# Memory attention and a routed feed-forward on eight cores: gram and scores in one product, q turned after its projection, the factor chain moved, VectorE evicting one gathered bank, four norms of the second half made ahead

## The chip, the cores and the metric

One Trainium2 chip, the program on all 8 cores, each core with its own two of the 16 sequences (4096 tokens of 1024 values) and all weights; no core talks to another. The metric is device microseconds of the slowest core. An engine names its queue here: PE is TensorE, PEld its weight load, DVE VectorE, ACT ScalarE, POOL GpSimd, SP SyncE.

## What is computed

```
x = x + attn(layernorm(x)) ; x = x + ffn(layernorm(x))

attn: q, k, v = x Wq', x Wk', x Wv' in 16 heads of 64; k normalised per head
  for each chunk of 64 tokens, with a memory M (64x64) per head:
    scores = q k' / 8, causal mask, softmax;  attn_out = softmax v
    chunk_out = attn_out + 0.1 * q M
    then for each token of the chunk: M = M - alpha (M k) k' + beta v k'
  out = concat(chunk_out) Wo'

ffn: tokens in groups of 16; for each of 64 experts the token of the group
     with the highest logit is chosen (0/1 matrix perm)
  sel = perm' x ; inner = relu(sel f1 + bias) ; inter = inner f2 ; out = perm inter
```

## The kernel before

**Attention (phase_a).** A step handles 128 rows: 64 tokens of each of the core's two sequences. The token recurrence of M is solved by chunk: gram (`gram`, -alpha k k') is masked by POOL into A[0] and B[0], nilpotent matrices whose powers PE makes by squaring (`power_a`, `power_b`, five and four products of 32 small 64x64 matmuls, all into PSUM psX, each copied out by ACT). DVE adds the identity (`plus_eye`, AI[k]) and PE multiplies them into W (`factor` 0 to 5, into psW, each copied out by DVE as W or, the last, Wf). `k_by_h`, `state_h` and `state_m` use and update the state H and M in psY. `scores`, exp, mask, `row_sums` and `values` are the softmax attention, also through psY, and `queries` adds q M. The projections of k, v and q and the output projection (`wo_part`) share the banks psD0 and psD1, as do the transposes of x and k (`x_turn`, `k_turn`, through psT, which is psD0).

The loop has 35 steps, i = -1 to 34, software-pipelined: in step i the projections belong to tile i, `gram` to tile i-1, powers, factors, scores and queries to u = i-2, and state and output projection to e = i-3. All engines are programmed by hand with semaphores; each executes its own list in order, so a wait holds all that is behind it. A projection half is 8 matmuls of 512 columns, except q, which was made with the weight as stationary operand: 64 matmuls of 128 columns, so that q comes out feature-major (q_fm) and needs no transpose. A weight load goes with each matmul ("pair" below).

PE's list of a full step before, in order: k half 0; power_a 1; factor 5 (e); k half 1; power_b 1; factor 0; state_h; v half 0; power_a 2; factor 1; state_m; half of v half 1; x_turn; power_b 2; k_by_h; rest of v half 1; power_a 3; factor 2; scores; q half 0; power_b 3; q half 1; factor 3; row_sums; gram; wo half 0; power_a 4; half of wo half 1; k_turn; power_b 4; queries; rest of wo half 1; power_a 5; factor 4; values. That is 834 pairs: 112 of projections, 16 of transposes, 2 of row sums and 22 groups of 32 small ones. POOL squares k, scales it, masks gram and scores, makes Pn and ka, and in between issues eight DMAs a step that cast the feed-forward weights f1, f2 to bf16 in DRAM.

**Feed-forward (phase_b).** Two halves of 16 tiles. A gather stage makes, for each tile, the layer norm (`choice_stats` and `choice_norm` on DVE, `choice_ln` on ACT), the transposed tile (`y_turn`, yf), logits, the choice matrix (perm, psel) and four gathers of 1024 columns into P0 and P1 in turn, which ACT alone evicts into R (L1070); gather q waits until copy q-2 is done. An expert stage runs 32 pairs of experts (`layer1`, relu, `layer2`; DVE and ACT evict a half each). A rows stage transposes R back, scatters, adds x1 and stores. Before, the norm of tile 16 and the statistics of tile 17 were made in the rows stage of the first half, and tiles 0 and 1 likewise at the end of attention.

## Time and profile before

| | us |
|---|---|
| median of 3 runs | 1457.8 (1455.39 to 1459.32) |
| profiled execution, time | 1463.14 |
| its span (slowest core, core 0) | 1460.0 |
| PE busy | 1176.9 (81%) |
| DVE busy | 959.4 (66%) |
| ACT busy | 814.2 (56%) |
| POOL busy | 686.8 (47%) |
| attention | 0 to about 1067 |
| gather, experts, rows of the first half | 1067 to 1150, to 1210, to 1265 |
| the same of the second half | 1265 to 1345, to 1402, to 1460 |

The page gives one execution, on its slowest core. Busy shares are averages over stages with different limits, so each stage is read for itself: which wait ends last there. An idle time put down to "issue" is one in which the engine waited for nothing that the profile shows. The first and last steps of attention stand apart from the full ones: the first wait for weights, the last have no projections.

### The profile page before, as it was taken

To read this page: it belongs to the slowest core of one execution; us is meant where nothing else is said; L and a number is where in the kernel's file an instruction comes from. 1 tells how busy PE (TensorE), PEld (TensorE's weight loads), DVE (VectorE), ACT (ScalarE), POOL (GpSimd) and SP (SyncE) were. 2 spreads that over 40 slices of the span, in tenths; PEclk is the share of its full clock that TensorE was granted. 3 is DMA by queue.
4 is the path that set the end of the run, shared out by engine and by line. 5 is a ranking of instruction groups with operands and counts; after the bars stand their busy time and mean duration, and the time that the engine had idled before them with its cause. 6 is when DMAs were issued, how large, how long until landed. Compare 5 with 4: busy or idle time off the path is not lost. (4 is left out here: it accounts for less than half of the span.)

```text
span 1460.0 us, 72310 instructions; the slowest of 8 cores (1445.7 to 1460.0 us)
## 1 busy us (share of the span) xinstructions
PE 1176.9 (81%) x31168; PEld 768.4 (53%) x31168; DVE 959.4 (66%) x1325; ACT 814.2 (56%) x1187; POOL 686.8 (47%) x566
## 2 busy tenths in 40 slices
PE   1578888888888988888888888885577879777788
PEld 0355565555555555555555555553444466543665
DVE  2266776676767777667765666765667467873776
ACT  0155555555555555555555555563339866489775
POOL 3176666766667666676666766676201000011000
PEclk9789999999999999999999999996558789888999
DMA  9812222222222222222222222113124285741958
GB/s 155 145 39 43 45 46 53 47 43 45 46 53 47 45 47 46 52 46 49 45 45 45 50 43 42 27 30 74 30 73 152 77 273 157 235 153 42 279 144 241
DMA packets 75173, 122.35 MB, mean 84 GB/s; under 512 B 13408, under 2 KB 38000, under 8 KB 74864
## 3 DMA queue, kind: packets, MB, share of 16 engines
q1 hardware_dynamic: 48128, 92.30, 21.1%
q0 software_dynamic: 26736, 25.44, 13.2%
q8 instruction: 254, 4.16, 1.2%
q14 instruction: 55, 0.45, 0.1%
HBM read 117.93 MB, written 41.94 MB: 110 GB/s over the span
## 5 line engine op out<-in xcount | busy, mean ns | idle before, releaser
L807 DVE CAST W<-psW 128x1024 bf16<-128x1024 f32 x160 | 195.1, 1219 | 100.5 <-PE psW L602 98.5
L403 ACT CAST B<-psX 128x1024 bf16<-128x1024 f32 x128 | 129.8, 1014 | 87.4 <-PE psX L570 87.4
L803 DVE TENSOR_TENSOR AI<-A,eye 128x1024 bf16<-128x1024 bf16 x160 | 118.5, 757 | 44.2 <-ACT A L399 43.1
L1058 POOL TENSOR_TENSOR psel<-permT_sb,gmask_sb 128x256 bf16<-128x256 bf16 x32 | 19.8, 620 | 269.3 <-DVE permT_sb L1287 244.1
L519 PE MATMUL psD<-xnf,wq_sb 128*128 128x128 bf16 x2048 | 132.7, 224 | 14.3 <-DMA wq_sb<-wqT 7.9
L486 PE MATMUL psD<-wk_sb,xnf 128*128 128x512 bf16 x512 | 128.8, 397 | 18.3 <-DMA wk_sb<-wkT 13.1
L399 ACT CAST A<-psX 128x1024 bf16<-128x1024 f32 x128 | 130.2, 1017 | 19.0 <-PE psX L570 18.8
L495 PE MATMUL psD<-wv_sb,xnf 128*128 128x512 bf16 x512 | 128.8, 385 | 13.0 <-DMA wv_sb<-wvT 11.7
L545 PE MATMUL psD<-wo_sb,o_fm 128*128 128x512 bf16 x512 | 131.9, 393 | 1.3 <-issue 1.0
L519 PEld LDWEIGHTS psD<-xnf,wq_sb 128*128 128x128 bf16 x2048 | 120.5, 100 | 19.0 <-issue 16.2
L358 POOL TENSOR_TENSOR Ms_sb<-M_sb,b 128x1024 bf16<-128x1024 bf16 x31 | 68.7, 2215 | 128.8 <-DVE M_sb L851 128.8
L1070 ACT CAST R<-P 128x1024 bf16<-128x1024 f32 x128 | 120.6, 1022 | 5.9 <-PE P L1148 5.5
L1297 DVE CAST R<-P 128x512 bf16<-128x512 f32 x128 | 81.6, 687 | 44.6 <-PE P L1175 44.4
L570 PEld LDWEIGHTS psX<-A,B 64*64 64x64 bf16 x5120 | 59.1, 111 | 96.2 <-issue 95.4
L602 PE MATMUL psW<-W,AI 64*64 64x64 bf16 x5120 | 80.1, 199 | 29.0 <-issue 21.3
L365 POOL TENSOR_TENSOR PT<-PT,mj 128x1024 bf16<-128x1024 bf16 x32 | 68.1, 2129 | 73.7 <-ACT PT L441 73.7
L570 PE MATMUL psX<-A,B 64*64 64x64 bf16 (+1 forms) x5120 | 77.8, 196 | 26.2 <-issue 11.9
L354 POOL TENSOR_TENSOR sq_sb<-kraw 128x1024 f32<-128x1024 f32 x32 | 60.7, 1896 | 76.4 <-ACT kraw L407 58.3
L411 ACT CAST vt<-psD 128x512 bf16<-128x512 f32 x64 | 37.5, 586 | 100.8 <-PE psD L495 100.8
L374 POOL TENSOR_TENSOR A<-g_sb,mlo 128x1024 bf16<-128x1024 bf16 x32 | 68.0, 2125 | 52.7 <-ACT g_sb L462 52.7
L807 DVE CAST Wf<-psW 128x1024 bf16<-128x1024 f32 x32 | 39.2, 1225 | 77.3 <-PE psW L602 77.3
L486 PEld LDWEIGHTS psD<-wk_sb,xnf 128*128 128x128 bf16 x512 | 46.8, 100 | 74.5 <-issue 29.2
(136 smaller groups left out, 2594.5 us busy)
## 6 DMA issues: line engine op xcount, KB each, us to landing
ring<-f1d SPq DMA_DIRECT2D x64, 256.0 KB, 4.0
ring<-f2d SPq DMA_DIRECT2D x64, 256.0 KB, 5.5
out<-ring SPq DMA_DIRECT2D x64, 256.0 KB, 4.0
xy<-x SPq DMA_DIRECT2D x68, 128.0 KB, 2.4
f1d<-f1w POOLq DMA_DIRECT2D x128, 64.0 KB, 2.5
f2d<-f2w POOLq DMA_DIRECT2D x128, 64.0 KB, 2.7
x1d<-x1b SPq DMA_DIRECT2D x64, 128.0 KB, 1.8
xy<-x1d SPq DMA_DIRECT2D x32, 256.0 KB, 3.1
```

The lines of the kernel that those rows point to most:

```text
L399: s.copy(A[k][:], psX[:, 0:1024]).then_inc(s_a, 1)
L403: s.copy(B[k][:], psX[:, 0:1024]).then_inc(s_b, 1)
L486: ins = t.matmul((psD0, psD1)[hf][:, :], xn_fm[i % 2][:, kc * 128:(kc + 1) * 128], wk_sb[:, kc * 1024 + hf * 512:kc * 1024 + hf * 512 + 51 ...
L495: ins = t.matmul((psD0, psD1)[hf][:, :], xn_fm[i % 2][:, kc * 128:(kc + 1) * 128], wv_sb[:, kc * 1024 + hf * 512:kc * 1024 + hf * 512 + 51 ...
L519: ins = t.matmul((psD0, psD1)[hf][:, (oc % 4) * 128:(oc % 4) * 128 + 128], wq_sb[:, kc * 1024 + oc * 128:kc * 1024 + oc * 128 + 128], xn_f ...
L545: ins = t.matmul((psD0, psD1)[hf][:, :], o_fm[:, oc * 128:(oc + 1) * 128], wo_sb[:, oc * 1024 + hf * 512:oc * 1024 + hf * 512 + 512], star ...
L570: ins = t.matmul(psX[c:c + 64, hr * 64:hr * 64 + width], left[k][r:r + 64, hr * 64:hr * 64 + 64], right[k][r:r + 64, hr * 64:hr * 64 + width],
L602: ins = t.matmul(psW[c:c + 64, hr * 64:hr * 64 + 64], AI[k][r:r + 64, hr * 64:hr * 64 + 64], w_old, start=True, stop=True, tile_position=( ...
L803: v.tensor_tensor(heads(AI[k][:, :]), heads(A[k][:, :]), by_mask(eye2), ALU.add).then_inc(s_ai, 1)
L807: v.tensor_copy((Wf if k == 5 else W[k % 2])[:], psW[:, 0:1024]).then_inc(s_w, 1)
L1070: s.copy(gather_place(n, q), P[q % 2][:, 0:1024].rearrange("p (h cb r) -> p h cb r", h=2, cb=4)).then_inc(s_ga, 1)
L1297: v.tensor_copy(place(2 * p)[:, 4 * hf:4 * hf + 4, :, :], half_tiles(P[u % 3][:, 0:512])).then_inc(s_iv, 1)
```

## The change

- **Gram and scores** become one group, `gram_and_scores(j)`, with j = i-1: k is the stationary operand and the moving one is 128 columns wide, 64 of -alpha k and 64 of q, from a joint buffer kaq. The result fills psX and psY together (psXY). ACT copies the even slots to g_sb and takes exp of the odd ones into PT, now two buffers, a step earlier than before. The group also waits for the turned q and for the logarithm of the row sums (s_lden), and power_a 4 and queries wait for the exp.
- **q** is projected as k and v are (16 matmuls of 512 columns), copied token-major to q_tm by ACT, transposed in `q_turn` (8 matmuls, through psD1) and copied to q_fm by DVE, which `wo_part` of half 1 and the next step's k half 1 wait for.
- **The factor chain** starts later: factors 0 to 3 run in step u+2, factors 4 and 5 in the next. PE's list of a full step after: k half 0; power_a 1; factor 4 (e); k half 1; power_b 1; factor 5 (e); v half 0; power_a 2; state_h; half of v half 1; power_b 2; state_m; rest of v half 1; x_turn; power_a 3; k_by_h; q half 0; power_b 3; factor 0; row_sums; half of q half 1; k_turn; gram_and_scores; factor 1; rest of q half 1; half of wo half 0; power_a 4; factor 2; q_turn; rest of wo half 0; power_b 4; queries; wo half 1; power_a 5; factor 3; values.
- **DVE's list** of a full step after: AI5 (e); evict factors 3 and 4; plus_eye 0; evict factor 5; plus_eye 1; H; the sum of squares kss (before, it stood behind factor 2, much later) and its maximum; M; xnf; plus_eye 2; RHS; stats of x; evict factor 0; k_fm; plus_eye 3; evict factor 1; normal (xn_tm); evict factor 2; q_fm; x1 half 0; plus_eye 4; x1 half 1.
- **At the end of attention** statistics and norms of tiles 0 to 3 are made (before: norm of 0, statistics of 0 and 1).
- **Gather**: ACT evicts gathers 0 to 2 whole and half of gather 3; DVE evicts the other bank of gather 3, at the end of its iteration, and PE waits for it before the next tile's gather 1.
- **Norms ahead**: in the first half's expert stage, between pairs 16 and 28, DVE and ACT make statistics and norms of tiles 16 to 19 (NPRE = 4), with their loads on SP among the weights; what stood in the rows stage is gone.

The diff, cut to its core (the lists of PE and DVE stand above in words; `o_copy` is the old copy of o_fm, now at the head of the next step):

```diff
-        q_fm = [sb(pa, f"qf{b}", [128, 1024]) for b in range(3)]
+        q_tm = sb(pa, "q_tm", [128, 1024])
+        kaq_fm = [sb(pa, f"kaq{b}", [128, 2048]) for b in range(3)]
-        ka_fm = [sb(pa, f"ka{b}", [128, 1024]) for b in range(3)]
-        PT = sb(pa, "PT", [128, 1024])
+        PT = [sb(pa, f"PT{b}", [128, 1024]) for b in range(2)]
-        psX = ps(pa, "psX", [128, 1024])
+        psXY = ps(pa, "psXY", [128, 2048])
-        psY = ps(pa, "psY", [128, 1024])
+        psX, psY = psXY[:, 0:1024], psXY[:, 1024:2048]
+        psT1 = psD1[:, :].bitcast(BF16)
+        gram_scores = psXY[:, :].rearrange("p (h b c) -> p h b c", b=2, c=64)
+        ka_fm = [kaq[:, 0:1024] for kaq in kaq_fm]
+        q_fm = [kaq[:, 1024:2048] for kaq in kaq_fm]
...
-                if 0 <= u < NT:
-                    g.wait_ge(s_exp, u + 1)
-                    g.tensor_tensor(heads(PT[:, :]), heads(PT[:, :]), by_mask(mj), ALU.mult).then_inc(s_ptm, 1)
...
+                    if u > 0:
+                        g.wait_ge(s_po, u)
+                    g.tensor_tensor(Pn[:], PT[u % 2][:], rden[:], ALU.mult).then_inc(s_pn, 1)
...
+                    cast(u, 6)
+                    g.wait_ge(s_exp, i)
+                    g.tensor_tensor(heads(PT[(i - 1) % 2][:, :]), heads(PT[(i - 1) % 2][:, :]), by_mask(mj),
+                                    ALU.mult).then_inc(s_ptm, 1)
...
-                if proj:
-                    v_half(i, 1)
-                if solve:
-                    power_a(u, 3)
-                    s.wait_ge(s_psc, u + 1)
-                    s.activation(PT[:], psY[:, 0:1024], AF.Exp, scale=0.125).then_inc(s_exp, 1)
                 if proj:
                     s.wait_ge(s_kmax, i + 1)
                     s.activation(rk[:], kss[:], AF.Ln).then_inc(s_rk, 1)
                     s.wait_ge(s_rk, 2 * i + 1)
                     s.activation(rk[:], rk[:], AF.Exp, scale=-0.5).then_inc(s_rk, 1)
+                    v_half(i, 1)
+                if solve:
+                    power_a(u, 3)
+                if proj:
                     q_half(i, 0)
                 if solve:
                     power_b(u, 3)
-                if i + 2 < NT:
-                    ln_steps(i + 2)
+                    s.wait_ge(s_pden, u + 1)
+                    if u > 0:
+                        s.wait_ge(s_pn, u)
+                    s.activation(rden[:], psY, AF.Ln).then_inc(s_lden, 1)
                 if i == -1:
                     s.wait_ge(s_const, NCONST)
                     s.activation(ab_sb[:, :], ab_sb[:, :], AF.Exp, scale=-1.0).then_inc(s_esig, 1)
+                if 0 <= j < NT:
+                    s.wait_ge(s_pg, j + 1)
+                    s.copy(heads(g_sb[:, :]), gram_scores[:, :, 0, :]).then_inc(s_g, 1)
+                    s.activation(heads(PT[j % 2][:, :]), gram_scores[:, :, 1, :], AF.Exp, scale=0.125).then_inc(s_exp, 1)
-                if solve:
-                    s.wait_ge(s_pden, u + 1)
-                    s.activation(rden[:], psY[:, 0:1024], AF.Ln).then_inc(s_lden, 1)
-                if 0 <= i - 1 < NT:
-                    s.wait_ge(s_pg, i)
-                    s.copy(g_sb[:], psX[:, 0:1024]).then_inc(s_g, 1)
                 if solve:
                     s.wait_ge(s_lden, u + 1)
                     s.activation(rden[:], rden[:], AF.Exp, scale=-1.0).then_inc(s_rec, 1)
+                if i + 2 < NT:
+                    ln_steps(i + 2)
+                if solve:
                     power_a(u, 4)
                     power_b(u, 4)
-                    s.wait_ge(s_po, u + 1)
-                    s.copy(o_fm[:, :].rearrange("p (a s c) -> p s a c", a=8, s=2),
-                           psY[:, 0:1024].rearrange("p (s a c) -> p s a c", s=2, a=8)).then_inc(s_o, 1)
                 if i >= NT + 1:
-                    choice_ln(s, env, i - NT - 1)
+                    choice_ln(s, env, 2 * (i - NT - 1))
+                    choice_ln(s, env, 2 * (i - NT - 1) + 1)
...
+                    if i > 3:
+                        t.wait_ge(s_x1, 2 * (i - 3) - 1)
                 else:
                     if i > 0:
-                        t.wait_ge(s_q, 2 * i)
+                        t.wait_ge(s_qfm, i)
...
-            def q_half(i, hf):
...
-                for oc in range(4 * hf, 4 * hf + 4):
-                    for kc in range(8):
-                        ins = t.matmul((psD0, psD1)[hf][:, (oc % 4) * 128:(oc % 4) * 128 + 128],
-                                       wq_sb[:, kc * 1024 + oc * 128:kc * 1024 + oc * 128 + 128],
-                                       xn_fm[i % 2][:, kc * 128:(kc + 1) * 128],
-                                       start=(kc == 0), stop=(kc == 7))
-                ins.then_inc(s_pq, 1)
+                for kc in range(lo, hi):
+                    ins = t.matmul((psD0, psD1)[hf][:, :], xn_fm[i % 2][:, kc * 128:(kc + 1) * 128],
+                                   wq_sb[:, kc * 1024 + hf * 512:kc * 1024 + hf * 512 + 512],
+                                   start=(kc == 0), stop=(kc == 7))
+                if hi == 8:
+                    ins.then_inc(s_pq, 1)
...
-                if i > 2:
-                    t.wait_ge(s_x1, 2 * (i - 3) + 1)
...
+            def q_turn(i):
+
+                t.wait_ge(s_q, 2 * i + 2)
+                for oc in range(8):
+                    ins = t.transpose(psT1[:, oc * 128:(oc + 1) * 128], q_tm[:, oc * 128:(oc + 1) * 128], ident_bf[:])
+                ins.then_inc(s_tq, 1)
...
                     t.wait_ge(s_o, e + 1)
-                    if e + 3 < NT:
-                        t.wait_ge(s_q, 2 * (e + 3) + hf + 1)
-                    else:
-                        t.wait_ge(s_kfm, NT)
+                    t.wait_ge((s_kfm, s_qfm)[hf], min(e + 4, NT))
+                    if e + 3 >= NT:
                         t.wait_ge(s_x1, 2 * e)
...
-            def gram(j):
+            def gram_and_scores(j):
+
                 t.wait_ge(s_ka, j + 1)
+                t.wait_ge(s_qfm, j + 1)
                 if j > 0:
                     t.wait_ge(s_b, 4 * (j - 1) + 3)
+                    t.wait_ge(s_lden, j)
                 for h in range(NH):
                     r, hr = (h % 2) * 64, hrow(h)
                     for s in range(2):
                         c = (h // 2) * 128 + s * 64
-                        ins = t.matmul(psX[s * 64:s * 64 + 64, hr * 64:hr * 64 + 64],
-                                       ka_fm[j % 3][r:r + 64, c:c + 64], k_fm[j % 3][r:r + 64, c:c + 64],
+                        ins = t.matmul(psXY[s * 64:s * 64 + 64, hr * 128:hr * 128 + 128], k_fm[j % 3][r:r + 64, c:c + 64],
+                                       kaq_fm[j % 3][:, :].rearrange("p (b x) -> p b x", b=2)[r:r + 64, :, c:c + 64],
                                        start=True, stop=True, tile_position=(r, s * 64))
...
                     t.wait_ge(s_g, u + 2)
+                    t.wait_ge(s_exp, u + 2)
...
-            def scores(u):
-                t.wait_ge(s_rhs, u + 1)
-                t.wait_ge(s_q, 2 * u + 2)
...
-                ins.then_inc(s_psc, 1)
-
             def row_sums(u):
                 t.wait_ge(s_ptm, u + 1)
+                t.wait_ge(s_rhs, u + 1)
...
                     load_pair(32 * half + p)
+                    if half == 0 and 16 <= p < 16 + NPRE:
+                        load_y(p)
...
-                    if half == 0 and 2 <= tl < 2 + NY:
-                        load_y(16 + tl - 2)
+                    if half == 0 and 2 <= tl < 2 + NY - NPRE:
+                        load_y(16 + NPRE + tl - 2)
...
-                s.copy(gather_place(n, q),
-                       P[q % 2][:, 0:1024].rearrange("p (h cb r) -> p h cb r", h=2, cb=4)).then_inc(s_ga, 1)
+                h = 1 if q == 3 else 2
+                s.copy(gather_place(n, q)[:, 0:h, :, :], gathered_ps(q)[:, 0:h, :, :]).then_inc(s_ga, 1)
...
+                    if half == 0 and 17 <= p < 17 + 3 * NPRE and p % 3 == 2:
+                        choice_ln(s, env, 16 + (p - 17) // 3)
...
+                if n > 0 and q == 1:
+                    t.wait_ge(s_gv, n)
...
+                t.wait_ge(s_gv, 16 * (half + 1))
...
-                    if j + 3 < 16:
+                    if NPRE <= j + 3 < 16:
                         choice_norm(v, env, n + 3)
...
+                    if 0 <= j - 2:
+                        v.wait_ge(s_pg, 4 * (n - 2) + 4)
+                        v.tensor_copy(gather_place(n - 2, 3)[:, 1, :, :], gathered_ps(3)[:, 1, :, :]).then_inc(s_gv, 1)
...
+                    if half == 0 and 16 <= p < 16 + 3 * NPRE and p % 3 == 1:
+                        choice_stats(v, env, 16 + (p - 16) // 3)
+                    if half == 0 and 18 <= p < 18 + 3 * NPRE and p % 3 == 0:
+                        choice_norm(v, env, 16 + (p - 18) // 3)
...
-                    if half == 0 and tl in (8, 10):
-
-                        choice_stats(v, env, 16 + (tl - 8) // 2)
-                    if half == 0 and tl == 13:
-                        choice_norm(v, env, 16)
```

## Rows read from the trace of the kernel before

**Rows 1.** Busy time by stretch: us, PE, PEld, DVE, ACT, POOL (instructions), PEclk, DMA, GB/s.
```profile
232.00:901.00 669.00, 577.37 (x18347) 376.57 (x18346) 463.26 (x550) 363.23 (x506) 451.20 (x352) 0.99 0.24 47
```

**Rows 2.** What PE waited for, 232 to 901 us: total us, times, longest.
```profile
PE psW L602 <- issue: 16.1, 22, 1.3
PE psX L570 <- issue: 15.7, 20, 1.5
...
PE psY L640 <- DVE M_sb L851: 6.5, 12, 0.6
PE psX L570 <- ACT g_sb L462: 6.1, 14, 0.5
...
PE psD L507 <- issue: 0.3, 1, 0.3
```

**Rows 3.** DMA queues, 232 to 901 us.
```profile
q8 instruction: 148, 2.42, 1.5%
```

**Rows 4.** Timeline of PE in one step: start, us, line, tiles, count, idle before.
```profile
511.73 0.26 PE L625 MATMUL psY<-Wf,RHS 64*64 64x64 bf16 x8 [0.95 <-issue]
...
515.85 0.43 PE L602 MATMUL psW<-W,AI 64*64 64x64 bf16 x29 [0.20 <-issue]
516.18 0.45 PE L652 MATMUL psY<-qf,kf 64*64 64x64 bf16 x32
516.56 1.96 PE L519 MATMUL psD<-xnf,wq_sb 128*128 128x128 bf16 x32
518.45 0.45 PE L570 MATMUL psX<-B,A 64*64 64x64 bf16 x32
520.76 1.95 PE L519 MATMUL psD<-xnf,wq_sb 128*128 128x128 bf16 x32 [1.86 <-issue]
...
527.20 0.61 PE L532 MATMUL psD<-ident_bf,kt 128*128 128x128 bf16 x8
527.74 0.45 PE L570 MATMUL psX<-B,A 64*64 64x64 bf16 x32
```

**Rows 5.** Timeline of ACT and DVE in the same step.
```profile
518.27 1.21 DVE L868 TENSOR_REDUCE kss<-sq_sb 128x16 f32<-128x1024 f32 x1
...
522.36 0.20 ACT L395 ACTIVATE rstd<-rstd 128x1 f32<-128x1 f32 x1
...
524.36 0.80 DVE L795 TENSOR_SCALAR xn_tm<-xy,mv,rstd 128x1024 bf16<-128x1024 f32 x1
524.64 1.01 ACT L462 CAST g_sb<-psX 128x1024 bf16<-128x1024 f32 x1
525.53 1.07 ACT L465 ACTIVATE rden<-rden 128x1024 f32<-128x1024 f32 x1
...
528.39 0.68 DVE L894 COPY kf<-psD 128x1024 bf16<-128x1024 bf16 x1
```

**Rows 6.** Timeline of attention's last step.
```profile
1054.43 1.23 DVE L807 CAST Wf<-psW 128x1024 bf16<-128x1024 f32 x1 [1.07 <-PE psW L602]
```

**Rows 7.** Costliest groups of the page: an eviction of one bank.
```profile
L1297 DVE CAST R<-P 128x512 bf16<-128x512 f32 x128 | 81.6, 687 | 44.6 <-PE P L1175 44.4
```

**Rows 8.** What PE waited for in the gather stage of the first half, 1085 to 1150 us.
```profile
PE P L1148 <- ACT R L1070: 12.1, 29, 0.7
```

**Rows 9.** Timeline of the first tiles of the first gather stage.
```profile
1074.11 0.68 DVE L117 BATCH_NORM_STATS2 bst_y<-xy 128x6 f32<-128x512 bf16 x1
...
1074.48 1.03 PE L1115 MATMUL P<-ident_bf,xy 128*128 128x128 bf16 x8 [2.67 <-DVE yf L1271]
```

**Rows 10.** Timeline late in the second gather stage's fill: an iteration of DVE.
```profile
1283.37 0.63 DVE L136 TENSOR_SCALAR xy<-xy,mv_y,rstd_y 128x1024 bf16<-128x1024 bf16 x1 [0.33 <-ACT rstd_y L130]
...
1287.50 0.56 DVE L136 TENSOR_SCALAR xy<-xy,mv_y,rstd_y 128x1024 bf16<-128x1024 bf16 x1 [0.40 <-ACT rstd_y L130]
```

**Rows 11.** Busy time of the first half's expert stage, columns as in rows 1.
```profile
1150.00:1210.00 60.00, 48.17 (x1032) 37.89 (x1032) 39.77 (x63) 44.61 (x98) 0.00 (x0) 0.84 0.70 213
```

**Rows 12.** Timeline of PE in the first half's rows stage.
```profile
1242.45 0.62 PE L1202 MATMUL P<-ring,pselT_sb 128*64 128x512 bf16 x4 [0.83 <-DVE ring L1303]
```

196 lines of the change are left out of this document (108 added, 88 removed).

## Prediction

> **What bounds the kernel now.** I read the page's slices first (attention is 1067 of 1460 us, PE eight or nine tenths busy), then the busy time of the 22 full steps between 232 and 901 us, then who PE waited for in them, the DMA queues of the same stretch, one step instruction by instruction, and last the stages of the feed-forward. A full step takes 669/22 = 30.4 us, and PE is busy for 577.4/22 = 26.2 of them; DVE is busy for 21.1, POOL for 20.5, ACT for 16.5 [rows 1]. So PE is the bound, but 4.2 us a step are idle. The table of waits says why: 13 of its rows, of which the two largest and the smallest stand, are "issue", together 67.1 us or 3.05 a step; all waits for other engines make about 20 us, 0.9 a step, the largest M_sb (6.5) and g_sb (6.1) [rows 2].
>
> What "issue" is comes out of two more views. The instruction queue moved 148 packets, 2.42 MB, so about 16 KB each, one every 669/148 = 4.5 us, and 18,347 pairs / 148 = 124 pairs of weight load and matmul go with each [rows 1, 3]. In the timeline the gaps stand at just that distance: from the end of the gap at 515.85 to the next come 29+32+32+32 = 125 pairs, in 4.9 us, and 4.1 us passed since the gap before [rows 4]. After slow pairs (projections of 512 columns) there is no gap, after quick ones there is. I read this as PE running out of instructions: a packet takes some 4.2 us (estimated from the two distances, 4.1 and 4.9, the lower weighing more because waits of other kinds lengthen some), and where 124 pairs take less work than that, PE waits.
> The Trainium skill, page "Runtime: NRT & Kernel Launch", section "Instruction fetch mechanics", says that engines are refilled in 16 KiB blocks of 256 instructions, and there the trace agrees (148 packets of 16 KB); it also says that this fetch is hidden because instructions issue slower than blocks arrive. The gaps of up to 2.4 us every 124 pairs speak against that, and by the page they would have another cause and stay; that is the last rival.
>
> **The change, attention.** *Work of PE in a full step.* q: 64 matmuls in two halves of 1.89 us become 16 of 512 columns; k's and v's halves take about 1.84, so -0.1. q_turn adds 8 transposes, 0.54 from the start of k_turn to what follows [rows 4]. Scores and gram, each 32 small matmuls in 0.38 us (516.18 to 516.56 [rows 4]), become 32 of 128 columns: not below one group (0.38), not much above two (0.76, the same columns), as far as the trace has a like; I take 0.6, nearer to the upper end because the columns are twice as many, so -0.16. Sum +0.3 (0.0 to +0.45): 26.5 us.
> *Instructions.* 48 pairs of q and 32 of scores go, 8 come: 834 becomes 762, or 6.73 packets a step 6.15. This is the gain. Before, work and outside waits per packet were (26.2+0.9)/6.73 = 4.0 us; after, (26.5+2.4)/6.15 = 4.7, 0.65 more. If each gap shrinks by 0.65, of the 87 gaps that I listed in the stretch (65.9 us in all, from 0.2 to 2.4) those beyond keep 21 us together, 0.95 a step instead of 3.05.
> *New waits.* From the end of gram_and_scores (call it 0) ACT copies g (1.0), takes exp (1.0), copies q half 1 (0.6), takes exp of rden (1.07), does ln (two short ones, 0.6 with their hand-over), then A4 (1.0) [rows 5]. With 0.2 us of hand-over A4 is done at 5.6, and behind it on PE stand power_b 4, queries and wo half 1. PE's own work up to there (factor 1, half of q, half of wo, power_a 4, factor 2, q_turn, half of wo) is 4.6. So 1.0 us is lost. Then DVE: normal can start only after ln (4.6), 0.8; eviction of factor 2, 1.2; q_fm, 0.7: wo half 1 gets its bank at 7.3 to 7.4, where PE is ready at 6.6. Another 0.75. In the first part of the step kss (1.2 and about 0.6 for the maximum) now stands ahead of M on DVE: k_by_h, and the q projection behind it through xnf, wait for M until about 12.4 of the step where PE arrives at about 11.2; about 1.3 with xnf. In all 3.1 us if PE is never held by anything else; before, such waits were halved by the fetch gaps that fell ahead of them, so I take 2.4 (0.9, as before, to 3.1). The other moves cost nothing: DVE has 21.1+0.7 of 30 us, hidden by PE's work; POOL's kt, Pn, B0 and the mask are ready by the walk at least 2 us early; ACT's work is the same. SP's loads of x wait for q copies that come about as before, three tiles ahead.
> *Sum.* 26.5+2.4+0.95 = 29.8, with joints 29.7, against 30.4: -0.7 us, times 30 full steps = **-21 us**. Ends: waits of 0.9 give 28.4, -2.0 a step, -60; all 3.1 give 30.4, nothing.
>
> *End of attention.* The last step now begins with the eviction of factor 3 and has factor 4 before factor 5: one more product of 0.9 and one more eviction of 1.2 in a chain in which DVE and PE wait for one another [rows 6]; +2. The exp of scores leaves the last solving step's chain, -1. Two more norms and two more statistics on DVE lie beside wo's products and the last store, +0.5. Together **+1.5** (-1 to +4).
>
> **The change, feed-forward.** *Fill of the gather stages.* With four norms ready, y_turn of tile 2 doesn't wait 2.67 us behind norm and statistics of DVE (two of 0.68 and an aggregate before each copy of yf) [rows 9]; with a little for tile 3, -4 in the first half, and -2.5 in the second, where one norm was ready already.
> *Evictions.* PE waited 12.1 us in 65 for ACT's copies [rows 8]. Only the waits behind gather 3 go, where ACT now needs 0.6 for 1.0; gather 0 waits for gather 2's whole copy as before. -0.25 for some 12 tiles a half at PE's low clock. But DVE gets 0.69 for its bank [rows 7]: its iteration of 4.1 us in the fast part, with some 0.4 idle [rows 10], becomes 4.4, and DVE takes ACT's place as the bound there: +0.3 for some 6 tiles of the second half. Last tiles of each half, without statistics, gain 0.4 four times. Together -5 (-12 to +3).
> *Expert stage.* Four statistics of 1.6 us and four norms of 0.55, 8.7 us of DVE work, fall into 12 of 32 pairs, some 22 us. DVE is busy 39.8 of 60 [rows 11], evenly 15 in those 22, so there is room for 7; but the evictions come in strict turn and the layer 2 buffers let DVE lag by one pair only. Ends 1.5 and 8.7; I take +4. SP's four loads among the weights hide, since the ring is ten pairs deep.
> *Rows stage.* The statistics held PE by 0.83 us, twice, of which one stands [rows 12]: **-1.7**.
> Sum of the feed-forward: -4-2.5-5+4-1.7 = **-9** (-18 to +3).
>
> **Total.** -21+1.5-9 = -28.5 us. Against the profiled execution's own 1463.1 (3.1 outside its span) that is 1434.6; this execution lies 5.3 above the median of 1457.8, so for the median I say **1429 us**.
>
> **Rivals.**
> *Full relief.* The waits in the step stay at 0.9, because the remaining gaps and other work cover ACT's chain: 28.4 a step, -60 +1.5 -9, about 1390 us. For it: before, g and M cost 0.3 each where their walk says 0.5 to 0.6. Against: two chains of 0.75 to 1.0 with no slack stand close together.
> *The chain takes it all.* Waits of 3.1 and gaps of 0.95: 30.4 a step, only the rest remains: about 1451.
> *Slower, by DVE's list.* kss stands ahead of M and waits for POOL's squares; M holds k_by_h, xnf and through it all of q. It decides from the point at which POOL's square ends later than H, about 2 us of slack by my walk; then each us of POOL's lateness is one of PE's, and normal's wait for ln does the same later in the step. With 1.5 us more, 31.2 a step: +24+1.5-7 = 1476. POOL's 20.5 us of 30.4 speak against it.
> *Slower, the gaps aren't the fetch.* Then they stay at 3.05: with 26.5 and 1.8 of waits 31.3 a step, +27+1.5-7, about 1479. The even distance of 124 pairs speaks against it. This is what the Trainium skill's rule on instruction fetch comes to here.
>
> **How the numbers follow.** Forecast 0.48 (its own range 1414 to 1445), full relief 0.22, the chain takes it all 0.13, slower by DVE 0.10, gaps not the fetch 0.07. The range of 1387 to 1456 holds the first three with their spreads and leaves out the slower two and a little below. A measurement of this kernel can tell about 0.3% from no change. Faster by more: 0.48+0.22 and two thirds of the third, 0.78; slower 0.16; within 0.3% the rest, 0.06.
>
> **What would show it.** Right: full steps of 29.7 us; the instruction queue at about 135 packets for 22 steps; "issue" near 1 us a step; on PE new waits for ACT's A4 before power_b 4 and for DVE's q_fm before wo; gram_and_scores in 0.5 to 0.7 us; fewer waits for R's copies in the gather; DVE without idle time in the middle of the first expert stage. Wrong: "issue" still 3 us a step; waits for M_sb over 1 us a step; a group of 128 columns of 0.85 us or more; a gather stage that is longer because PE waits for DVE's bank.

## The result: 54 us slower, all of it in attention

| | before | after |
|---|---|---|
| median of the runs, us | 1456.6 | 1510.9 |
| range of the runs, us | 1452.8 to 1459.3 | 1508.0 to 1512.5 |
| profiled execution, own time / span, us | 1463.1 / 1460.0 | 1511.1 / 1509.5 |
| last half of x1 starts (end of attention), us | 1064.7 | 1130.9 |
| from there to the end, us | 395.3 | 378.6 |
| one full step of attention, us | 30.5 | 33.1 |

The ratio is 1.037 (95% interval 1.0348 to 1.0392). All times and ratios here and below are of the fast runs: some executions of any kernel run some per cent longer, with a lower granted clock on the cores of one die, and are left out. A step is here the mean distance between two starts of GpSimd's first mask, `A<-g_sb,mlo`, between 230 and 930 us; all steps below are measured so. Attention grew by 66 us, where the forecast took 19.5 off it, and the feed-forward shrank by 17, where the forecast took 9. Most of what follows is about the 66.

Page of the kernel after, the costliest groups (busy us, mean ns of one, idle before):

```profile
L824 DVE TENSOR_TENSOR AI<-A,eye 128x1024 bf16<-128x1024 bf16 x160 | 271.0, 1694 | 1.3 <-ACT A L410 1.3
...
L568 PE MATMUL psD<-wo_sb,o_fm 128*128 128x512 bf16 x512 | 139.4, 410 | 50.6 <-DVE kaq L917 50.6
```

The same instruction, plus_eye, is line 803 of the kernel before, where its row in the groups reads:

```profile
L803 DVE TENSOR_TENSOR AI<-A,eye 128x1024 bf16<-128x1024 bf16 x160 | 118.5, 757 | 44.2 <-ACT A L399 43.1 <-POOL A L374 1.0
```

The shape, the count and the operands are the same, yet one takes 1694 ns instead of 757. No part of the change touches it except its place.

Busy time of the kernel after in the stretch of [rows 1], with the same columns; what PE waited for in it, as in [rows 2]; and the instruction queue, as in [rows 3]:

```profile
232.00:901.00 669.00, 550.16 (x15387) 310.51 (x15385) 557.69 (x524) 338.57 (x468) 408.70 (x324) 0.95 0.22 43
```

```profile
PE psD L568 <- DVE kaq L917: 37.4, 20, 2.1
PE psXY L596 <- DVE AI L857: 26.9, 20, 1.9
PE psW L629 <- DVE W L828: 16.0, 21, 0.8
PE psXY L596 <- ACT A L410: 7.4, 16, 0.6
PE psXY L667 <- DVE M_sb L879: 5.8, 15, 0.7
PE psW L629 <- issue: 4.6, 9, 1.0
PE psXY L596 <- issue: 4.0, 8, 1.0
```

```profile
q8 instruction: 125, 2.05, 1.3%
```

Per step (22.0 of them before, 20.2 after, from 762 pairs a step):

| us a step | before | forecast | after |
|---|---|---|---|
| PE busy | 26.2 | 26.5 | 27.2 |
| issue | 3.05 | 0.95 | 0.68 |
| waits for other engines | 0.9 | 2.4 | 4.9 |

So the relief came: issue rows sum to 13.7 us in place of 67.1. That they are even smaller than forecast isn't a gain by itself, since a wait for an engine hides an instruction packet that arrives in it. What ate the relief is the third line of the table, and of its 98.5 us in the stretch 80.3 are three waits for VectorE: for q's turned copy (37.4), for the fifth AI (26.9), for an eviction of psW (16.0).

Where VectorE's time went is seen in one step. Timeline of VectorE, GpSimd and TensorE after the copy of A4 (start us, duration us, engine and line, out<-in, idle before):

```profile
500.43 2.14 POOL L383 TENSOR_TENSOR Pn<-PT,rden 128x1024 bf16<-128x1024 bf16 x1 [0.28 <-ACT rden L483]
...
500.88 2.23 DVE L816 TENSOR_SCALAR xn_tm<-x,mv,rstd 128x1024 bf16<-128x1024 f32 x1 [2.04 <-ACT rstd L406]
...
503.03 1.21 DVE L828 CAST W<-psW 128x1024 bf16<-128x1024 f32 x1
503.23 2.13 POOL L386 TENSOR_TENSOR B<-g_sb,mup 128x1024 bf16<-128x1024 bf16 x1
504.17 0.68 DVE L917 COPY kaq<-psD 128x1024 bf16<-128x1024 bf16 x1
504.76 0.67 DVE L835 TENSOR_TENSOR x1b<-xy,psD 128x512 bf16<-128x512 f32 x1
504.99 3.31 PE L568 MATMUL psD<-wo_sb,o_fm 128*128 128x512 bf16 x8 [1.60 <-DVE kaq L917]
505.29 0.55 POOL L354 DMA_DIRECT2D f2d<-f2w  x1
505.36 5.03 DVE L824 TENSOR_TENSOR AI<-A,eye 128x1024 bf16<-128x1024 bf16 x1
...
505.85 2.13 POOL L389 TENSOR_TENSOR PT<-PT,mj 128x1024 bf16<-128x1024 bf16 x1
507.93 1.89 POOL L395 TENSOR_TENSOR kaq<-kf,nega 128x1024 bf16<-128x1024 bf16 x1
...
510.31 0.67 DVE L835 TENSOR_TENSOR x1b<-xy,psD 128x512 bf16<-128x512 f32 x1
```

Normal takes 2.23 us where [rows 5] has 0.80, and ends 0.54 after GpSimd's Pn. plus_eye 4 takes 5.03 where 0.68 is usual, and ends 0.57 after GpSimd's last multiply (507.93 + 1.89 = 509.82 to 510.39). The evictions in between, whose input is in PSUM, have their usual 1.21 and 0.68 beside GpSimd's B. Between 232 and 901 us plus_eye takes over 2 us in 20 instances, one in each step, all of 5.02 to 5.04, and it is plus_eye 4 each time. Behind it the second half of x1 and the fifth AI are late, so are product 5 of psX and the eviction of factor 3. In this step PE has waited 1.60 us, and behind the wait its granted clock falls from the 2.4 to about the 1.2 GHz level: the eight products of wo take 3.31 us, for 1.89 of eight like ones at the full level. Busy time of these 3.2 us, columns as before, with 0.55 as the granted clock (it is 1.00 in the 7 us ahead of them):

```profile
505.00:508.20 3.20, 3.20 (x8) 0.94 (x8) 3.20 (x2) 0.00 (x0) 3.19 (x4) 0.55 0.34 67
```

This doesn't follow every wait. The same wait stands in all 20 steps (1.2 to 2.1 us); behind it wo's products take 3.16 to 3.43 us in six of them and 1.89 in fourteen. The clock also falls behind the wait for the fifth AI, in twelve steps. Over the whole stretch it is 0.95, for the 0.99 of [rows 1].

### The profile page after: what moved, and what is told of

It reads as the page before. It is cut to its first block and busy times, and to the rows that moved or that the text cites. A ratio compares the mean times of both kernels' runs of the same rounds, so it can differ in the third digit from the quotient of the medians.

```text
span 1509.5 us, 68111 instructions; the slowest of 8 cores (1491.9 to 1509.5 us)
## 1 busy us (share of the span) xinstructions
PE 1193.4 (79%) x28864; PEld 704.3 (47%) x28864; DVE 1155.3 (77%) x1389; ACT 809.9 (54%) x1187; POOL 677.6 (45%) x566
## 3 DMA queue, kind: packets, MB, share of 16 engines
q1 hardware_dynamic: 48128, 92.30, 19.5%
## 5 line engine op out<-in xcount | busy, mean ns | idle before, releaser
L824 DVE TENSOR_TENSOR AI<-A,eye 128x1024 bf16<-128x1024 bf16 x160 | 271.0, 1694 | 1.3 <-ACT A L410 1.3
L414 ACT CAST B<-psXY 128x1024 bf16<-128x1024 f32 x128 | 129.8, 1014 | 57.5 <-PE psXY L596 57.4
L410 ACT CAST A<-psXY 128x1024 bf16<-128x1024 f32 x128 | 129.3, 1010 | 48.9 <-PE psXY L596 48.7
L539 PE MATMUL psD<-wq_sb,xnf 128*128 128x512 bf16 x512 | 128.7, 385 | 11.7 <-DMA wq_sb<-wqT 6.8
L365 POOL TENSOR_TENSOR kt<-kraw,rk 128x1024 bf16<-128x1024 f32 x32 | 61.2, 1913 | 128.8 <-ACT rk L460 128.8
L1108 ACT CAST R<-P 128x1024 bf16<-128x1024 f32 (+1 forms) x128 | 110.0, 906 | 8.4 <-PE P L1187 6.4
L596 PE MATMUL psXY<-A,B 64*64 64x64 bf16 (+1 forms) x5120 | 74.7, 194 | 50.3 <-DVE AI L857 41.4
L596 PEld LDWEIGHTS psXY<-A,B 64*64 64x64 bf16 x5120 | 57.4, 110 | 111.0 <-issue 107.4
L629 PE MATMUL psW<-W,AI 64*64 64x64 bf16 x5120 | 76.9, 199 | 33.8 <-DVE W L828 29.3
L418 ACT COPY kraw<-psD 128x512 f32<-128x512 f32 x64 | 37.4, 586 | 117.0 <-PE psD L507 117.0
L568 PEld LDWEIGHTS psD<-wo_sb,o_fm 128*128 128x128 bf16 x512 | 49.2, 103 | 107.2 <-issue 68.1
L596 PEld LDWEIGHTS psXY<-B,A 64*64 64x64 bf16 x4096 | 49.0, 114 | 80.7 <-issue 80.5
```

What stands on the lines that cost most here:

```text
L410: s.copy(A[k][:], psX).then_inc(s_a, 1)
L414: s.copy(B[k][:], psX).then_inc(s_b, 1)
L539: ins = t.matmul((psD0, psD1)[hf][:, :], xn_fm[i % 2][:, kc * 128:(kc + 1) * 128], wq_sb[:, kc * 1024 + hf * 512:kc * 1024 + hf * 512 + 51 ...
L568: ins = t.matmul((psD0, psD1)[hf][:, :], o_fm[:, oc * 128:(oc + 1) * 128], wo_sb[:, oc * 1024 + hf * 512:oc * 1024 + hf * 512 + 512], star ...
L596: ins = t.matmul(psX[c:c + 64, hr * 64:hr * 64 + width], left[k][r:r + 64, hr * 64:hr * 64 + 64], right[k][r:r + 64, hr * 64:hr * 64 + width],
L629: ins = t.matmul(psW[c:c + 64, hr * 64:hr * 64 + 64], AI[k][r:r + 64, hr * 64:hr * 64 + 64], w_old, start=True, stop=True, tile_position=( ...
```

## The experiments

Theory (the **meeting**): a VectorE instruction that takes its inputs from SBUF stands still as long as GpSimd works on SBUF, through several of GpSimd's instructions if they follow closely. The change moved normal, plus_eye 4 and GpSimd's mask of PT into one another. Rivals: the new operand waits themselves (**waits**: A4, q's copy, the order of VectorE's list), or the new shapes and tiles. The Trainium skill, page "SBUF — State Buffer", section "Who interferes with whom", has the mechanism as a rule: VectorE and GpSimd share one pair of SBUF ports, taken as an exclusive lock, and an instruction of VectorE with two SBUF inputs contends with a GpSimd one that reads SBUF, as does a copy or tensor_scalar in a two-port mode with GpSimd. Both kinds that stretched here are of its list: plus_eye has two inputs in SBUF (0.68 us alone, 5.03 here), and normal is a tensor_scalar from SBUF to SBUF (0.80 and 2.23). In which mode normal ran, no trace shows.

All rows below named "group" are of the list of costliest groups, the waits are those of PE between 232 and 901 us. e1 to e8 were measured on one chip, e9 and e10 on a second, e11 and e12 on a third; the kernel before, run beside them, took 1457, 1453 and 1457 us. A difference between two chips is therefore given below by the ratios to the kernel before as well. Summary:

| run | edit | us | step us |
|---|---|---|---|
| e1_mask_short | after, mask of PT left out but for one head | 1448.1 | 30.8 |
| e2_eye4_late | after, plus_eye 4 behind x1's second half | 1492.5 | 32.0 |
| e3_norm_early | after, ln and normal earlier | 1484.1 | 33.3 |
| e4_both | e2 and e3 | 1518.4 | 33.1 |
| e7_eye4_next | after, plus_eye 4 one step on | 1454.7 | 30.7 |
| e6_no_meeting | e7 and e3 | 1439.1 | 30.4 |
| e9_pool_waits | e6, GpSimd held back | **1393.9** | 28.9 |
| e12_eye0_too | e9, plus_eye 0 earlier as well | 1405.9 | 29.4 |
| e8_more_pairs | e6, 96 pairs a step more | 1465.1 | 31.1 |
| e5_before_ffn | before, feed-forward part alone | 1451.7 | 30.5 |
| e10_before_meets | before, plus_eye 4 beside GpSimd | 1607.9 | 35.5 |
| e11_before_held | e10, GpSimd held back | 1492.9 | 31.9 |

**e1_mask_short** leaves the causal mask of 15 of 16 heads out (so the scores of these aren't masked):

```diff
-g.tensor_tensor(heads(PT[(i-1)%2]), heads(PT[(i-1)%2]), by_mask(mj), ALU.mult)
+g.tensor_tensor(PT[(i-1)%2][:, 0:64], PT[(i-1)%2][:, 0:64], mj[:, :], ALU.mult)
```

> The changed kernel, but POOL masks only one head of PT (64 of 1024 columns), so the causal mask is left out for the rest; every wait stays. Theory A (VectorE operations that read two SBUF tiles, or one in a fast mode, can't run while POOL reads SBUF): plus_eye 4, 5.0 us in the changed kernel, becomes about 2.9, and a full step gets 1 to 1.8 us shorter, about 1465 us. Theory B (only the new order of waits costs: normal behind ln, q_fm behind normal, M behind kss): nobody waits late for this mask, so plus_eye 4 and the time stay, 1511 us.

1448.1 us, one run, 63 less than the kernel after and 17 less than expected. The group of plus_eye falls to a mean of 964 ns, and plus_eye 4 takes 0.68 us in every step of the stretch, though VectorE's list is untouched; I had expected 2.9. Work was removed, so this only shows that GpSimd's list stretches VectorE; the wait for q's copy stays, since normal still lies beside Pn:

```profile
L824 DVE TENSOR_TENSOR AI<-A,eye 128x1024 bf16<-128x1024 bf16 x160 | 154.3, 964 | 1.3 <-ACT A L410 1.3
```

```profile
PE psD L568 <- DVE kaq L917: 38.8, 21, 2.1
```

**e2_eye4_late**, **e3_norm_early** and **e4_both** move VectorE's instructions within the step:

```diff
 # e2: VectorE                     # e3: VectorE
 x1_half(e, 0)                     k_fm copy
-plus_eye(u, 4)                    +normal(i + 2)
 x1_half(e, 1)                     plus_eye(u, 3); factor(u, 1)
+plus_eye(u, 4)                    -normal(i + 2)
                                   # and on ScalarE ln_steps(i + 2) ahead of g's copy
```

> The changed kernel with plus_eye 4 moved on VectorE behind the second x1 half; nothing left out. Theory A: it meets only the end of POOL's ka, takes about 1.2 us instead of 5.0, while x1's second half waits for PE anyway; AI5 comes 0.7 us earlier a step, about 1490 us. Theory B: no change or slower, 1511 to 1520, since the same work stands in the same list.

> The changed kernel with ln on ACT directly behind rden's logarithm and normal on VectorE directly behind k_fm, ahead of plus_eye 3, so before POOL starts A0; nothing left out. Theory A: normal takes 0.8 instead of 2.24 us, no wait of 2.2 us for ln stands on VectorE, q_fm is there when PE wants it (wait of 1.9 us a step gone), about 1440 us. Theory B: the wait goes too but normal's duration is the same as before the move; 1460 to 1480 us.

> The changed kernel with both moves, plus_eye 4 behind the second x1 half and ln and normal early; nothing left out. Theory A: attention steps near 29.5 us, 1415 to 1430 us in all, below the kernel before. Theory B: no better than the early norm alone.

1492.5, 1484.1 and 1518.4 us. e2 took the time expected, though plus_eye 4 did not: it takes 1.1 to 2.8 us, 2.0 on average, for 1.2. In e3 normal is back at 0.81 us and the wait for q's copy is gone, but the time fell by 27 only, not by 71: plus_eye 4, which now starts 2.6 us earlier behind gram_and_scores, meets three instructions of GpSimd (B, PT, the scaling of k) in place of two and takes 7.5 us in most steps. Its profile (an execution of 1493.8 us) holds a test of its own: the 20 steps in which plus_eye 4 takes 7.3 to 7.6 us last 31.8 to 35.0 us, the eight in which it takes 0.7 to 1.3 last 26.8 to 30.0. And of the eight cores, with the same work each, the one with 12 such meetings between 232 and 901 us has the shortest span (1443.2) and the two with 17 and 18 the longest (1492.3 and 1487.3). Groups of e3, and its largest wait:

```profile
L824 DVE TENSOR_TENSOR AI<-A,eye 128x1024 bf16<-128x1024 bf16 x160 | 304.1, 1901 | 1.3 <-ACT A L410 1.3
```

```profile
PE psXY L596 <- DVE AI L857: 57.6, 18, 4.1
```

e4, expected at 1415 to 1430, was slower than the kernel after: behind x1 plus_eye 4 still meets the mask and the scaling (4.83 us at 528.59), now later in the step. Both misses have one cause: I moved the instruction by its old durations, to where GpSimd had been, and GpSimd's list moved along. No place that I tried inside this tail of GpSimd's multiplies was safe.

**e7_eye4_next** and **e6_no_meeting** put plus_eye 4 into the next step, ahead of the eviction of factor 4 (PE's waits for AI count accordingly, as in all runs below that move it); e6 also has e3's edit.

```diff
-if solve: plus_eye(u, 4)
 # next step
 factor(e, 3)
+plus_eye(e, 4)
 factor(e, 4)
```

> The changed kernel with the move of plus_eye 4 alone, ln and normal where the change has them. Theory A: the waits for AI5 and W go (2 us a step), the wait for q_fm (1.9 us a step) stays, since normal still meets Pn for 2.24 us and waits for ln: 1440 to 1460 us. Theory B: 1500 or more.

> The changed kernel, nothing left out: ln and normal early as in e3, and plus_eye 4 moved into the next step between the evictions of factors 3 and 4, when POOL has done ka and has nothing until the squares of k. Theory A (VectorE's two-input and fast SBUF operations wait while POOL reads SBUF): plus_eye 4 takes 0.7 us in every step, steps are 28 to 29 us as in the steps of e3 in which they don't meet, 1395 to 1420 us in all, below the kernel before. Theory B (VectorE's order and load as such): factor 4 now waits for one more operation of VectorE, no better than e3 at its best, 1450 or more.

1454.7 us (ratio to before 0.9984, 0.9945 to 1.0023) and 1439.1 (0.9852, 0.9816 to 0.9889). One instruction moved gives back the whole loss of the change, 56 of 54 us: in e7 plus_eye 4 takes 0.79 us on average, while the wait for q's copy stays (40.9 us in the stretch). e6 is faster than both kernels, but 19 us above its expectation, and its trace says why: without normal's delay VectorE comes earlier and plus_eye 4 meets GpSimd's tail again, with 2.8 us on average and 3.4 at most. The 16 us between e7 and e6 aren't normal's stretch alone, since e3's edit also takes a wait of about 2 us for ln off VectorE's list; no run parts the two. Waits of e6, largest row, and timeline:

```profile
PE psW L629 <- DVE AI L824: 35.4, 20, 2.6
```

```profile
505.82 2.14 POOL L389 TENSOR_TENSOR PT<-PT,mj 128x1024 bf16<-128x1024 bf16 x1
...
507.39 2.97 DVE L824 TENSOR_TENSOR AI<-A,eye 128x1024 bf16<-128x1024 bf16 x1
...
507.90 1.90 POOL L395 TENSOR_TENSOR kaq<-kf,nega 128x1024 bf16<-128x1024 bf16 x1
```

**e9_pool_waits** leaves VectorE as in e6 and moves GpSimd instead, by one wait:

```diff
 cast(u, 6)
 g.wait_ge(s_exp, i)
+if 0 <= u < NT: g.wait_ge(s_ai, 6 * u + 6)   # plus_eye 4 done
 g.tensor_tensor(heads(PT[...]), ...)          # the mask, then the scaling of k
```

> As e6_no_meeting, and GpSimd holds its mask of PT and the scaling of k back until VectorE's plus_eye 4 is done, so that no GpSimd work lies beside that instruction; the same instructions on every engine, GpSimd has one wait more a step. Theory (a VectorE instruction with inputs in SBUF is stretched by GpSimd work beside it): plus_eye 4 takes 0.68 instead of 2.97 us, the product behind it starts 2.3 us earlier, the clock's dip behind it goes, so 1.3 to 2.5 us less in each of 30 steps than e6's 1439: 1365 to 1410, likeliest 1395. Theory that e6 is already held by something else (the operand waits as such): within 10 us of 1439. If GpSimd's delayed list comes to set the end (scaling of k needed by gram_and_scores, some 16 us later): over 1450.

1393.9 us, ratio 0.959 (0.9549 to 0.963): 45 us below e6 (38 by the ratios, 0.985 to 0.959) and 4.1% below the kernel before, for one added wait. The rival of the operand waits, within 10 us of 1439, is out. This is the cleanest test in the changed kernel: the same instructions on every engine, VectorE's and TensorE's in the same order. Busy time, the largest waits, and plus_eye 4 with GpSimd behind it:

```profile
232.00:901.00 669.00, 600.58 (x17607) 348.59 (x17605) 535.89 (x603) 382.39 (x533) 471.77 (x370) 0.99 0.24 48
```

```profile
PE psXY L669 <- DVE M_sb L882: 13.4, 20, 3.3
PE psXY L654 <- DVE H_sb L872: 11.9, 16, 2.0
PE psW L631 <- DVE W L830: 10.5, 19, 2.4
```

```profile
510.74 0.68 DVE L826 TENSOR_TENSOR AI<-A,eye 128x1024 bf16<-128x1024 bf16 x1
...
511.57 2.12 POOL L391 TENSOR_TENSOR PT<-PT,mj 128x1024 bf16<-128x1024 bf16 x1 [2.10 <-DVE AI L826]
```

With 23.1 steps in the stretch PE works 26.0 us a step, waits 0.9 for instructions and 1.8 for engines. The clock is back at 0.99. Not every meeting is gone: plus_eye 0, 1 and 2 take 1.3 to 1.6 us on average here, for the 0.68 of an undisturbed one.

**e12_eye0_too** tried to free plus_eye 0 as well, which takes 2.02 us at 514.07 in e9 beside the scaling of k.

```diff
 plus_eye(e, 4)
+plus_eye(u, 0)
 factor(e, 4)
-plus_eye(u, 0)
 # GpSimd waits for 6 * u + 7
```

> As e9_pool_waits, and plus_eye 0 (which met the scaling of k there, 2.02 us) stands right behind plus_eye 4, ahead of the eviction of factor 4, in time in which VectorE waited for TensorE (1.51 us); GpSimd waits for both. Theory of the meeting: it takes 0.68, the last eviction and the adding to H come up to 1.3 us earlier, TensorE's waits for H (11.9 us, 16 times in 669 us) and M (13.4, 20) shrink: 0.3 to 1 us a step below e9's 1394, 1362 to 1386. Rival: these waits are set by the chain of products itself, then within 5 us of 1394.

1405.9 us, 12 slower than e9 (8 by the ratios, 0.965 and 0.959, whose intervals overlap), where 8 to 32 less were expected: a miss for both theories as I had put them. The timeline shows the meeting moved, not gone. GpSimd, held for one instruction more, gets to k's scaling and the square later, and in several steps plus_eye 1, which stands ahead of the adding to H, lands beside the square:

```profile
489.09 3.23 DVE L826 TENSOR_TENSOR AI<-A,eye 128x1024 bf16<-128x1024 bf16 x1
...
489.85 1.90 POOL L361 TENSOR_TENSOR sq_sb<-kraw 128x1024 f32<-128x1024 f32 x1
...
492.24 1.21 DVE L873 TENSOR_TENSOR H_sb<-H_sb,psXY 128x1024 bf16<-128x1024 bf16 x1
...
493.59 0.45 PE L654 MATMUL psXY<-Wf,RHS 64*64 64x64 bf16 x32 [1.47 <-DVE H_sb L873]
```

That this makes up the difference isn't shown. Over the run plus_eye takes less than in e9 (a mean of 1068 ns for 1145), and PE's waits for H, M and W in the stretch sum to 37.4 us for 35.8. Why e12 isn't faster stays open.

**e10_before_meets** and **e11_before_held** take the question into the kernel before, with nothing of the change. e10 moves plus_eye 4 behind the fifth AI; e11 is e10 with GpSimd's B and scaling of k held until plus_eye 4 is done.

```diff
 # e10, VectorE                      # e11 adds, GpSimd
-plus_eye(u, 4)   # behind x1 half 0   cast(u, 6)
 AI[5] += eye                        +g.wait_ge(s_ai, 6 * u + 6)
+plus_eye(u, 4)                        B <- g_sb by mup
 factor(u, 4)
```

> The kernel before with one instruction moved: VectorE's plus_eye 4 stands behind the fifth AI (about 502.4 in its trace) where GpSimd's B and ka run (501.3 to 505.3), instead of behind the first half of x1, where GpSimd is idle or issues a DMA. Nothing of the change is in it. Theory: plus_eye 4 takes 2.5 to 3.2 us there, the mean of the AI<-A,eye group rises from 757 ns to 1150 to 1300, and the fourth eviction is 3 to 4 us later, so 1 to 3 us a step: 1490 to 1540. Theory that the stretch comes with something of the change (the shared tile of ka and q, two PT tiles, the order of the other instructions): plus_eye 4 stays at 0.7 us and only the lost head start is paid, 1460 to 1490.

> As e10_before_meets (the kernel before, plus_eye 4 behind the fifth AI), and GpSimd holds B and ka back until plus_eye 4 is done. VectorE's and TensorE's lists are those of e10, so the lost head start of plus_eye 4 is paid in both and only the meeting is gone. Theory of the meeting: plus_eye 4 back at 0.68 us (4.42 in e10), TensorE's wait for it from 5.2 us a step to about 1.5, some 3.7 us a step and 30 steps less than e10's 1608: 1480 to 1510. Theory that the late place of the instruction, not its length, costs e10's 155 us: within 20 us of 1608.

1607.9 us (ratio 1.1053) and 1492.9 (1.0233). Groups and waits of e10, then of e11:

```profile
L803 DVE TENSOR_TENSOR AI<-A,eye 128x1024 bf16<-128x1024 bf16 x160 | 215.5, 1363 | 2.3 <-ACT A L399 1.3 <-POOL A L374 1.0
```

```profile
PE psW L602 <- DVE AI L803: 98.6, 19, 5.7
```

```profile
L805 DVE TENSOR_TENSOR AI<-A,eye 128x1024 bf16<-128x1024 bf16 x160 | 110.7, 708 | 2.3 <-ACT A L401 1.3 <-POOL A L374 1.0
```

```profile
PE psW L604 <- DVE AI L805: 34.7, 21, 1.8
```

The late place, with GpSimd held, costs the kernel before 36 us, the meeting 115 more (119 by the ratios). e11 is within its range. The wait for plus_eye 4 falls from 5.2 to 1.65 us each, 3.5 a step, and the step from 35.5 to 31.9. e10 came out 68 us above its range; one term was too small: I had 2.5 to 3.2 us for the stretched instruction, from one neighbour and a part of the next, and it takes 3.1 to 4.6 in all 20 steps, 4.2 on average, with a clock of 0.91. So a rival that ties the stretch to the change's shared tile or shapes is out.

**e8_more_pairs** tests the other half of the prediction, the instruction packets: e6 with 96 more pairs of weight load and matmul a step for the same columns.

```diff
-for kc in range(8): matmul(psD[hf][:, :], xn_fm[kc], wk_sb[512 columns])
+for c in range(4): for kc in range(8): matmul(psD[hf][:, 128 columns], xn_fm[kc], wk_sb[128 columns])
 # the same for half 0 of v and q
```

> The kernel e6 with k's both halves, v's first and q's first projected in 128 columns instead of 512: the same columns, 96 more pairs of load and matmul a step (858 instead of 762, the kernel before had 834). If PE is held by instruction packets of 124 pairs, the issue waits come back, from under 1 to about 3 us a step, and the time rises by 40 to 70 us. If the gaps have another cause, it rises by 0.2 us a step, 6 us in all.

1465.1 us, 26.0 more than e6, well above the 6 of the rival and below the 40 to 70 of the packets. Issue rows go from 18.9 to 33.2 us in the stretch, 0.7 us a step more, where some 2 were expected; the packets of the whole run go from 237 to 261, and PE's work per step from 26.6 to 27.0 us. So the direction is right and the size too small. A likely reason, not tested: both kernels wait 1.6 to 1.8 us a step for plus_eye 4, in which packets arrive unseen.

**e5_before_ffn** is the kernel before with only the feed-forward part of the change (four norms ahead, VectorE's bank of gather 3, statistics in the expert stage).

> The kernel before with the feed-forward part of the change alone (VectorE evicts one bank of gather 3, tiles 0 to 3 and 16 to 19 normalised ahead); attention as before. My prediction had -9 us for it; the two traces say about -16, since from the end of attention to the end before took 392.6 us and after 375.9. So 1440 to 1450 us beside 1457. If it is near 1457, the gain seen in the trace after comes from another state of the clock.

1451.7 us, ratio 0.9954 (0.9929 to 0.998), so 3 to 10 us by the timed runs, a little less than expected; its one profile is shorter by 14.4 behind the last x1 (395.3 to 380.9). The other traces narrow this down, since each run has one of the two feed-forward parts. From the last x1 to the end the three traces with the old part (before, e10, e11) take 395.3, 391.3 and 390.0 us, the eleven with the new one 378.6 to 388.0, with a median of 380.9: about 10 us by the medians.

## Why the prediction was wrong

**What bounds the kernel: right.** PE with its instruction packets. Issue fell from 3.05 to 0.68 us a step (0.89 in e9, whose other waits of 1.8 us hide less; 0.95 were forecast for 2.4), 834 to 762 pairs gave 6.2 packets a step where 6.15 were forecast, and putting pairs back (e8) put issue time back. The rival by which the gaps stay at 3.05 is out. What the runs show is that this idle time goes with the number of pairs; that the packets cause it rests on the even distance of the gaps. The Trainium skill's statement, page "Runtime: NRT & Kernel Launch", section "Instruction fetch mechanics", that fetching is hidden, doesn't fit these runs.

**PE's work: right, but for the clock.** The product of 32 by 128 columns took 0.44 us (0.6 forecast):

```profile
528.90 0.64 PE L585 MATMUL psXY<-kaq,kf 64*64 64x128 bf16 x32 [0.17 <-ACT rden L471]
529.34 0.45 PE L629 MATMUL psW<-W,AI 64*64 64x64 bf16 x32
```

from its start to the next group's. In e9, at the full clock, a step's work is 26.0 us, 0.5 under the forecast. In the kernel after it is 27.2, at a clock of 0.95.

**New waits: two too dear, one too cheap, two not named.** A4 cost 7.4/20.2 = 0.4 us a step (1.0 forecast), M and xnf 0.4 (1.3). q's copy cost 1.85 (0.75). The fifth AI, which the prediction didn't name at all, cost 1.3, and the eviction of psW 0.8.

**The step that failed** is the sentence "The other moves cost nothing: DVE has 21.1+0.7 of 30 us, hidden by PE's work", and with it normal at "0.8" in the sum of new waits. Both carry durations from the trace of before into places where GpSimd's neighbours are different. By the groups, plus_eye grew by 152.5 us over the run (118.5 to 271.0) and normal by 39.1 (its two groups 26.8 to 65.9), 6 us a step; 4.2 of them are plus_eye 4 and 1.4 normal, both in the tail of the step where q's copy, x1 and the fifth AI stand in one line on VectorE. Of the 98.5 us of waits in the stretch 80.3 lie behind these. For q's copy the sum can be followed: in each step normal starts 4.12 us behind the end of gram_and_scores, 0.5 earlier than forecast, but takes 2.24 us for 0.8, and the copy ends at 8.1 where 7.3 to 7.4 was forecast. Of GpSimd the prediction asked only whether its results would come in time, and they did; it didn't ask what GpSimd does beside VectorE. Moving plus_eye 4 by itself took 56 us back (e7), normal and ln with it 16 more (e6), holding GpSimd back 38 to 45 more (e9).

The trace of before had the sign, in its last steps and, small, in the very step that I had read. Before, VectorE and GpSimd in both places:

```profile
1017.18 2.15 POOL L378 TENSOR_TENSOR Pn<-PT,rden 128x1024 bf16<-128x1024 bf16 x1
...
1017.66 4.85 DVE L803 TENSOR_TENSOR AI<-A,eye 128x1024 bf16<-128x1024 bf16 x1 [0.81 <-ACT A L399]
...
1019.27 0.54 POOL L347 DMA_DIRECT2D f2d<-f2w  x1
...
1019.83 2.13 POOL L381 TENSOR_TENSOR B<-g_sb,mup 128x1024 bf16<-128x1024 bf16 x1
```

```profile
525.79 2.13 POOL L374 TENSOR_TENSOR A<-g_sb,mlo 128x1024 bf16<-128x1024 bf16 x1 [2.57 <-ACT g_sb L462]
...
527.61 0.86 DVE L803 TENSOR_TENSOR AI<-A,eye 128x1024 bf16<-128x1024 bf16 x1 [0.98 <-ACT A L399]
```

Both plus_eye end 0.55 us behind GpSimd's last multiply (1021.96 to 1022.51, 527.92 to 528.47). 160 instances of one shape with a median of 685 ns and a longest of 4850 ask for a reason, and the reason would have priced the move.

**The rivals.** "Slower, by DVE's list" (0.10) had the right engine and the wrong mechanism: it saw kss ahead of M and normal's wait for ln, and priced 1.5 us a step by lateness of an input; M cost 0.3. "Full relief" at 1390 is close to what the change gives with most of the meeting gone: e9 has 1393.9. The agreement is partly luck. Its step of 28.9 us lies between the 28.4 of that rival and the 29.7 of the forecast, its attention ends 53 us earlier than before where the rival has 58.5, and its feed-forward is 15 shorter in that trace where the forecast has 9; it also has plus_eye 4, normal and ln in other places and one wait more. So the relief that the sum took off is there, but only in another order of the lists.

**End of attention** can't be told apart from the late steps in these traces.

**Feed-forward: -9 forecast, -16.7 in the two profiles, -3 to -10 timed in e5, about -10 over all traces.** *Fill*: the first four turns of y take 6.5 us (1133.80 to 1140.26) for 10.2 before (1067.61 to 1077.84); forecast -4, measured -3.8. *Evictions*: PE's waits ahead of the gather's products, both halves, are 29.3 us for 29.4: ScalarE's fell, VectorE's came, as the prediction feared, and its -5 isn't there as waits. Groups of after, PE behind the end of attention:

```profile
L1187 PE MATMUL P<-psel,xy 64*128 64x256 bf16 x512 | 57.8, 306 | 29.3 <-ACT R L1108 23.7 <-DVE R L1334 5.1
...
L1241 PE MATMUL P<-ring,pselT_sb 128*64 128x512 bf16 x256 | 39.8, 390 | 2.2 <-ACT ring L1144 2.2
```

*Experts*: the waits of both layers sum to 22.8 us for 23.4, of which 7.5 (2.4 and 5.1) are new ones for VectorE, so the statistics cost near nothing net (+4 forecast). *Rows*: 2.2 for 3.9, the forecast -1.7. All PE waits there sum to 68 us for 75; the rest of the 16.7 is busy time, 337 for 346, spread over all products, which differs with the granted clock between two executions. That it belongs to the change isn't shown. Over the fourteen traces the feed-forward gains about 10 us, close to the forecast of 9.

## What to carry to other kernels

A duration read from a trace belongs to its neighbours as well as to its shape. Before moving an instruction of VectorE that reads SBUF, write down what GpSimd does at the new place, and look for instances of the same shape whose longest is a multiple of the median: they show what a meeting costs. Where the two can't be kept apart by order, let the engine with slack wait: one wait on GpSimd was worth 38 to 45 us here, and took back 115 of what e10 had cost in the kernel before.
